# A sixteen-sequence stack of attention, int8, Mamba and fp4 layers on one core: the lag of the state's turn, its timetable, and the place of the weight preparation

## The reference

```python
# layer 0, attention: 16 heads of 16 features, chunks of 64
A = einsum('bhcf,bhsf->bhcs', q_i, k_i) ** 2 * mask
o = (inter_o + A @ v_i) / (inter_z + A.sum(-1) + EPS)
# layer 0, network: weights are int32 of the range -127..127, times 1/127
h = silu(x @ Wg.T) * (x @ Wu.T);  x + h @ Wd.T
# layer 1, Mamba, forward in time and backward in time, 512 inner channels, 16 states
u  = silu(causal_conv4(x @ Win_u) + convb)
dt = softplus((u @ Wx_dt) @ Wdt + bdt);  B, C = u @ Wx_B, u @ Wx_C
h_t = exp(dt_t * A) * h_{t-1} + (dt_t * u_t) * B_t          # along 512 tokens
y = (sum_n h[n] * C[n] + u * D) * silu(z);  out = y @ Wout
# layer 1, network: fp4 of activations and of weights, block scale = max|x| / 6
h = silu(q4(x) @ q4(Wg).T) * (q4(x) @ q4(Wu).T);  x + q4(h) @ q4(Wd).T
```

## Times and profile before

| | us |
|---|---|
| median of three executions | 6630.95 |
| their range | 6627.23 to 6632.68 |
| the profiled execution | 6625.01 |
| span of its trace | 6623.3 |
| first scan starts | 281.1 |
| last scan starts | 6507.4 |

### The profile page before, as it was taken

How to read it: one execution, slowest core, us unless ns; L and a number is a source line. 1 busy time by engine, 2 the same in 40 slices (tenths; PEclk the granted TensorE clock), 3 DMA queues, 4 the chain that set the end, 5 groups by cost and what they waited for, 6 DMA issues and landing times. The chain is left out here.

```text
span 6623.3 us, 79907 instructions
## 1 busy us (share of the span) xinstructions
PE 4595.8 (69%) x21853; PEld 2953.3 (45%) x21900; DVE 4712.6 (71%) x6052; ACT 4210.5 (64%) x7080; POOL 4672.7 (71%) x2442
## 2 busy tenths in 40 slices
PE   5666677676777777676776777777677776767565
PEld 3344354443544444354443544444354444544443
DVE  4467686777768677686777768677686777768774
ACT  3476666667666666666667666666666667666562
POOL 0377767777777777767777876777777777776784
PEclk7787888888888888898888888888898888888777
DMA  3111111111111111111111111111111111111110
GB/s 114 37 36 47 42 52 41 52 46 34 58 40 47 43 54 50 39 50 42 51 46 34 60 38 47 46 50 51 39 50 43 52 44 40 54 39 42 43 44 27
DMA packets 152786, 308.71 MB, mean 47 GB/s; under 512 B 20870, under 2 KB 58310, under 8 KB 149926
## 3 DMA queue, kind: packets, MB, share of 16 engines
q1 hardware_dynamic: 152278, 302.80, 14.4%
HBM read 285.90 MB, written 16.84 MB: 46 GB/s over the span
## 5 line engine op out<-in xcount | busy, mean ns | idle before, releaser
L762 POOL TENSOR_TENSOR arena_m<-bS,arena_m 128x1024 f32<-128x1024 f32 x1024 | 2413.3, 2367 | 454.5 <-DMA bS<-brow 248.1
L1267 DVE TENSOR_TENSOR_SCAN arena_m<-psum,arena_m 128x512 f32<-128x512 f32 x2048 | 2437.4, 1209 | 161.1 <-ACT psum L990 125.3
L1564 PE MATMUL psum<-ident,arena_m 128*128 128x128 f32 x8192 | 1466.2, 316 | 1177.2 <-ACT hc L998 965.0
L1564 PEld LDWEIGHTS psum<-ident,arena_m 128*128 128x128 f32 x8192 | 1096.9, 162 | 1820.6 <-issue 1020.9
L990 ACT ACTIVATE psum<-arena_m,Aneg 128x512 f32<-128x512 f32 x2048 | 1414.6, 697 | 718.2 <-DVE arena_m L1267 695.3
L773 POOL TENSOR_TENSOR arena_m<-arena_m,hc 128x1024 f32<-128x1024 f32 x512 | 1212.8, 2369 | 460.2 <-ACT hc L998 354.7
L1278 DVE SCALAR_TENSOR_TENSOR arena_m<-psum,Ct,arena_m 128x512 f32<-128x512 f32 x1024 | 754.0, 737 | 681.3 <-PE psum L1564 679.0
L998 ACT ACTIVATE hc<-psum,Ct 128x512 f32<-128x512 f32 x1024 | 696.4, 680 | 38.9 <-PE psum L1564 38.6
L859 ACT ACTIVATE arena_a<-psum 128x512 f32<-128x512 f32 (+3 forms) x1024 | 380.3, 441 | 465.3 <-PE psum L1377 303.9
L1377 PE MATMUL psum<-arena_a 64*128 64x512 f32 (+3 forms) x2048 | 467.2, 562 | 160.0 <-ACT arena_a L859 56.4
L708 POOL TENSOR_SCALAR_AFFINE_SELECT arena_a<-arena_a 128x512 f32<-128x512 f32 x256 | 159.2, 637 | 540.5 <-ACT arena_a L859 540.5
(11 more groups left out here) (140 smaller groups left out, 7113.6 us busy)
## 6 DMA issues: line engine op xcount, KB each, us to landing
bS<-brow SPq DMA_DIRECT2D x512, 256.0 KB, 3.3
wB<-kept_B SPq DMA_DIRECT2D x16, 1408.0 KB, 6.2
wU<-kept_U SPq DMA_DIRECT2D x32, 512.0 KB, 5.6
wO<-kept_O SPq DMA_DIRECT2D x32, 512.0 KB, 5.7
wU<-kept_Z SPq DMA_DIRECT2D x32, 512.0 KB, 5.4
wA<-kept_A SPq DMA_DIRECT2D x16, 768.0 KB, 5.7
wB<-kept_B SPq DMA_DIRECT2D x16, 768.0 KB, 5.8
wA<-kept_A SPq DMA_DIRECT2D x16, 640.0 KB, 3.9
```

Source lines behind the costliest of these rows:

```text
L762: pool.tensor_tensor(hb[s % HBS][:, two, :], bS[:, s % 2, :].unsqueeze(1).to_broadcast([P, 2, T]), du[r][:, two, :], ALU.mult).then_inc(m_ ...
L1267: dve.tensor_tensor_scan(v, EB[j % EBS], v, 0.0, ALU.mult, ALU.add).then_inc(m_scan.sem, 1)
L1564: ins = pe.transpose(HT[i % 2][:, m * P:(m + 1) * P], hb[s % HBS][:, m, i * P:(i + 1) * P], ident[:, :])
```

## The change

`TURN` is 7 instead of 6: transposes, both additions to y and ACT's weighing stand one slot later behind the scan. All rows of the timetable are replaced by others. The weight preparation moves out of the program's start: SP loads the norm's vectors, x and the attention's weights first, then, at the end of sequence -2, all other weights and vectors. The casts, all transposes and their evictions and the fp4 quantisation, now one operation at a time over 44 slots, are spread over sequence -1, beside the first sequence's attention. The number of transposes, evictions, quantising operations and bytes is the same. The diff, cut:

```diff
-    TURN = 6
+    TURN = 7
...
-        row("d_turn", 1, -1, PE=[3.1, 3.2, 7, 7])
-        row("d_gate", 1, -1, DVE=[7, 7, 9, 9])
-        row("d_out", 1, -1, PE=[10.1, 11, 12, 13.1], DVE=[11, 14])
-        row("p_rows", 1, 0, SP=[26])
-        row("p_c", 1, 0, PE=[32], DVE=[33])
-        row("p_dt", 1, 0, PE=[35, 38, 41.3, 44], ACT=[36, 40, 42, 45], DVE=[37, 39, 43, 47], POOL=[39, 43, 44, 48])
-        row("z_in", 0, 0, PE=[45, 46, 48, 48], ACT=[46, 47, 48, 49])
-        row("q_silu", None, -1, ACT=[91, 98.1, 103, 108])
-        row("q_down", None, -1, PE=[101, 106, 112.1, 118], DVE=[101, 107, 113, 119])
-        row("a_v", None, 2, PE=[122, 123], DVE=[122, 124])
-        row("l_g1", None, -1, SP=[86])
-        row("l_x", None, 2, SP=[87])
+        row("d_turn", 1, -1, PE=[4, 5, 9.1, 9.2])
+        row("d_gate", 1, -1, DVE=[7, 7, 9, 9])
+        row("d_out", 1, -1, PE=[10.2, 11, 12, 13], DVE=[11, 14])
+        row("p_rows", 1, 0, SP=[54])
+        row("p_c", 1, 0, PE=[34], DVE=[38])
+        row("p_dt", 1, 0, PE=[35, 37, 41, 44], ACT=[37, 40, 43, 45], DVE=[38, 40, 43, 46], POOL=[36, 41, 45, 51])
+        row("z_in", 0, 0, PE=[44, 45, 47, 53.1], ACT=[46, 47, 51, 56])
+        row("q_silu", None, -1, ACT=[94.1, 97, 103, 109])
+        row("q_down", None, -1, PE=[101, 105, 112.1, 116], DVE=[102.3, 108, 116, 120])
+        row("a_v", None, 2, PE=[119, 125], DVE=[123, 127])
+        row("l_g1", None, -1, SP=[93])
+        row("l_x", None, 2, SP=[98])
...
-        FRONT, FP4_IN, FP4_DVE, FP4_PE, FP4_OUT, FREE = 0, 2, 12, 36, 56, 92
+        INT8_OUT, MAMBA_OUT, FP4_OUT, KEPT, FREE = 0, 40, 66, 77, 92
+        CASTS = (4, 5, 6)
+        JOB_SLOT = list(range(6, 6 + NJ8)) + list(range(28, 28 + NJ - NJ8)) + [44, 45, 46, 47, 48, 49, 50, 51] + [57, 57, 58, 58, 59, 59]
+        FP4_SLOT = [10 + q * 43 // (6 * QOPS) for q in range(6 * QOPS)]
+        DECAYS = 45
...
+                    if second(b) and j == SLOTS - 1:
+                        load_weights()
...
-            for n in range(NJ):
-                turn_weights(n)
             pe.wait_ge(const_set.sem, 5 + G)
-            pe.wait_ge(setup_act.sem, NJ // 2)
-            pe.wait_ge(setup_dve.sem, (NJ + 1) // 2)
...
-                    if first(b) and 0 <= j - FP4_PE < NJ4 - NJ:
-                        turn_weights(NJ + j - FP4_PE)
+                    for n in turned_in(b, j):
+                        turn_weights(n)
```

More of the change, by code:

```diff
@@ new lines, in block_kernel @@
+        row("d_turn", 0, 0, PE=[67, 69, 72.1, 72.2])
+        row("d_gate", 0, 0, DVE=[68, 70, 73.2, 74])
+        row("i_turn", 1, 0, PE=[70, 70.1, 73, 73], ACT=[70, 70, 75, 77])
+        row("f_up", None, 1, PE=[71, 72, 74, 74, 76, 76], DVE=[73, 73.1, 75, 77, 77, 78])
+        row("f_silu", None, 1, ACT=[73, 78])
+        row("d_out", 0, 0, PE=[78, 79, 80, 82], DVE=[79, 81.1])
+        row("f_down", None, 1, PE=[78, 79, 82, 82], DVE=[80, 84])
+        row("m_stat2", None, 1, ACT=[86], DVE=[81, 85, 86])
@@ L424, in first, with second @@
             return isinstance(b, int) and b == -1
+        def second(b):
+            return isinstance(b, int) and b == -2
         def take_bank(pe, b, piece, r, n):
```

305 lines of the change are left out of this document (159 added, 146 removed).

## The result

The changed kernel takes 6570.74 us (median of three, 6557.66 to 6581.83) against 6630.95. The ratio to before is 0.9909 with an interval of 0.9885 to 0.9932. A second set of five runs, beside other kernels on one chip, gave 6565.97 and 0.9909 (0.9895 to 0.9922). So it is 0.9% faster, some 60 us, where 121 us were forecast (6510, range 6440 to 6605). The time lies in the range; the gain is half of what I named, and the half that is missing is one term, the timetable. The profiled execution took 6581.8 us, 11 above the median.

What follows compares the result with a forecast made beforehand. Engines waiting for each other, none full, were taken to bound the kernel. From the profiled 6625.0 us, prelude -44, tail +3 and timetable -80 gave 6504; with 5.9 for the median the forecast was 6510 us, range 6440 to 6605.

Steps and rivals of the forecast that it cites:

- the timetable: Steady sequences: new slots gain 19.5 us a sequence, halved to 9.7, less 4.7 lost; net -5.0, or -80 over 16 sequences.
- The front: Program start: first statistics 28.2 us earlier, 4 taken off for PE's low clock; gain 24 us, between 21 and 28.
- The attention phase: First sequence's attention: loses PE's 27.8 us gap, takes on the set-up; 102.1 us becomes 82, gain 20 (7 to 30).
- The sum with POOL's ports: Prelude: spread quantising contends with POOL's masks over shared ports, up to 10 us, giving 6520; left out of the forecast.
- The lag: State turns one slot later behind the scan: costs 0, at most 2 us a sequence, and frees nothing by itself.
- The tail: From the last scan to the end: last states are turned a slot later, 3 us more.
- z_in: Steady sequences: no longer in four neighbouring slots, where DVE waited 6.66 us at an addition; credited 3 us a sequence.
- a_v: Side piece: four and two slots from maker to user instead of 0 and 1; its 5.5 us wait loses 3.5.
- p_c: Side piece, second direction: PE 34 to DVE 38 instead of 32 to 33; 4.81 us wait, credited 4 a sequence.
- q_up and p_dt: Side pieces with more room between maker and user: credited 2.5 of 8.1 and 4 of 8.4 us a sequence.
- the losses: Steady sequences: four or five places with lost leads, some 4 us each at a quarter, together 4.7 us a sequence.
- only the prelude gains: Rival, chance 0.21: the state's own waits take up what side pieces free; slot stays at 3.04 us, total 6590.

## Why the prediction was wrong, point by point

**What bounds the kernel** was read rightly as waits between engines, but as a sum of waits on DVE. Two things are missing. DVE's idle time is not made of terms that can be taken away one by one: it is 1635 to 1653 us between first and last scan in before, in the changed kernel and in the fastest version. And the instructions' own durations aren't fixed: TensorE is granted 0.85 on the mean and moves between two levels within a sequence, and VectorE's small operations take 0.16 us or up to 2.3 by what GpSimd does beside them.

**The front**: right in kind, 27.3 us at the scores instead of 24. The statistics came 29.1 us earlier instead of 28.2, and the stretch from there to the scores grew from 21.7 to 23.6 us, by 1.8 where I had taken 4 off for a low clock. That the clock would be low at first was right: L1365 takes 3.75 us at 14.28 and 1.89 at 25.00. The size was too large, since the clock was full from some 18.4 us on.

**The attention phase**: right. From the first scores to the first scan it is 18.5 us shorter, 20 forecast (7 to 30), and the whole prelude 45.8 in one profile and 43.1 in the other, 44 forecast. The gap of 27.8 us that I took away is the spread's 26.6. With the old timetable behind it the new prelude is worth 49.7, so an agreement to 1.8 us is partly luck. The sum with POOL's ports, set beside it at 10 us, wasn't needed: the 54 quantising operations took 45.8 us in the burst and 46.2 spread, with POOL busy beside them for 3.4 and 13.4 us. In the steady sequences, of which the prediction didn't say this, VectorE's small operations are held up by GpSimd's.

**The lag**: neutral within 0.3%, as argued (0.9919 against 0.9922). What the text didn't see is that the new timetable depends on it, for 315 us.

**The tail**: wrong in sign. It shrank by 8.1 us instead of growing by 3. It is 107.8 to 111.1 us in the traces with most of the new timetable and 115.8 to 117.3 in those with the old one, so the last sequence's late pieces do better in their new slots. The lag alone did lengthen it, by 1.5 us of the 3 (115.8 to 117.3).

**The timetable**: this is the step that failed. "The net is -5.0 us a sequence" measured +0.7 in the first profile (10.7 / 16), -0.7 in the second, and -0.2 by the medians of the run without the prelude (3 / 16). The cause of the miss is that a wait taken away at a line was counted as time gained: 155 us of waits went at three lines and DVE's idle time fell by 18. Its parts: z_in was right in size (38 us of 48). a_v was right in sign (31 of 56) as long as p_c stood late. p_c was wrong in sign: I priced a lead by the wait that it removes on the taking engine, and did not ask who next needs the PSUM bank that lies full meanwhile, though the kernel has only three for its side pieces. How much of the 24 us is that bank's, the clock's or VectorE's beside GpSimd is open. q_up and p_dt, credited with 6.5 us a sequence, kept their waits. And the losses were counted only where I had noticed a lost lead. The largest at one line, 77 us more waiting at the attention's division, stood at a part one of whose four leads had shrunk from a slot to none: there the wait went from nothing to 3.8 us a sequence. Slots 64 to 79, 10 us a sequence longer than before, were not priced at all. Halving the sum of the gains didn't help, because the terms are neither independent nor bounded by their waits. The two ends of this term are also wrong by its own figures: half of 19.5 with no losses is -9.7, not -9, and a third of 19.5 with the losses at twice 4.7 is +2.9, not +1.5.

The rival "only the prelude gains", at 6590 with a chance of 0.21, is what happened; of the 20 us below it 9 to 11 are the tail, and executions differ by the rest. Its reason is half right: PE's wait for `hc` fell by 266 us, but POOL's rose by 227 (354.7 to 581.8) and the one at the addition to y by 9, and other side pieces took up the rest. No run settles how much of the 80 us went to which: in two neighbouring sequences of one execution the clock makes up to 3.6 us and VectorE's small operations 5.0, together more than the whole term.

The fastest version is the changed kernel with p_c of the second direction on DVE at 35 and a_v at 120 and 126: 0.9862 (0.9847 to 0.9877) in one set and 0.986 in another, some 92 us faster than before and 32 faster than the change.

## What to carry to other kernels

Work that stands ahead of the first useful instruction, or in a burst ahead of an operation that another engine waits for, can be priced from the trace to a few microseconds; 44 us forecast, 45.8 measured. Slots moved in a timetable of four engines that are each some 70% busy can't be priced by adding up waits: ask of every lead which bank or buffer it holds longer and who takes that next, and then measure one row at a time. Where the granted clock moves within a period, compare equal stretches of several periods first; if the same instructions differ by 10%, that spread is larger than most of what one wants to find. Compare then the durations on every engine, not on TensorE alone: the most visible difference need not be the largest. And read a mean clock only where the trace has a record of it.
